# A second wait ahead of the indirect gathers in the hop loops of a graph kernel: Pool also waits for DVE's scores of the fifth group in front

## The reference, cut to what matters

```python
def agg(emb):
    a_input = jnp.concatenate([emb[head], emb[tail]], axis=-1)
    h = a_input @ fc_w.T + fc_b
    e = jnp.sum(h * rel_e, axis=-1)
    e = jnp.where(e > 0, e, LEAKY_SLOPE * e)
    m = jax.ops.segment_max(e, head, num_segments=N)
    ex = jnp.exp(e - m[head])
    denom = jax.ops.segment_sum(ex, head, num_segments=N)
    w = ex / denom[head]
    agg_emb = jax.ops.segment_sum(emb[tail] * w[:, None], head, num_segments=N)
    return agg_emb + emb
```

## Time and profile before

| What | Value |
|---|---|
| Runs shown | 9002.51 us median (8999.1 to 9027.76) |
| Time of the profiled execution | 8987.15 us |
| Its span, first to last instruction | 8985.1 us |
| Mean granted clock of PE | 0.782 of full speed |
| Busy share | PE 71%, DVE 54%, Pool 56%, ACT 25% |
| First and last gather of the hops (line 1305) | 2668.8 and 7368.5 us |
| Gathers of the hops | 2448 (3 x 408 x 2), 949 ns each |

### The profile page before, as it was taken

The page is one execution under the profiler, slowest core; times in us unless marked ns, Lnnn a source line. Parts: engine busy times, 40 slices in busy tenths (PEclk is TensorE's granted clock), DMA queues, the critical chain, the costliest instruction groups (busy, mean ns, idle before and its releaser), DMA issues. The chain is left out here.

```text
span 8985.1 us, 218235 instructions
## 1 busy us (share of the span) xinstructions
PE 6358.8 (71%) x51897; PEld 4355.0 (48%) x51899; DVE 4817.6 (54%) x20582; ACT 2235.8 (25%) x5532; POOL 5032.8 (56%) x4831
## 2 busy tenths in 40 slices
PE   2972888888208777788777588777787874666665
PEld 0110111111107666677666477666676763555554
DVE  7897555555315555555555555555555554333334
ACT  2000000000004444344444244434444431111111
POOL 2888777777764555455545355445455542555553
PEclk9985999999657888778888678788877775665655
DMA  3971666666223322223232233322222321222222
GB/s 124 310 233 41 195 186 191 186 186 192 44 49 82 83 82 82 80 83 83 82 80 80 63 81 83 82 80 81 81 84 81 83 61 38 48 47 48 47 47 40
DMA packets 573339, 882.86 MB, mean 98 GB/s; under 512 B 212594, under 2 KB 471113, under 8 KB 523997
## 3 DMA queue, kind: packets, MB, share of 16 engines
q10 hardware_dynamic: 76307, 411.51, 13.6%
q1 hardware_dynamic: 342522, 266.26, 11.2%
q0 software_dynamic: 154448, 204.37, 10.7%
HBM read 853.52 MB, written 20.36 MB: 97 GB/s over the span
## 5 line engine op out<-in xcount | busy, mean ns | idle before, releaser
L1305 POOL DMA_INDIRECT rows<-tab_d,stage_idx x2448 | 2322.7, 949 | 2378.7 <-PE ps_g L1369 1378.6
L232 POOL DMA_INDIRECT rec_d<-stage_rec,stage_row x1600 | 1967.5, 1230 | 648.8 <-issue 640.3
L440 PE MATMUL ps_gate<-ring,h_sb 128*1 128x512 f32 x3072 | 1530.8, 607 | 3.8 <-issue 3.6
L1332 PE MATMUL ps_t<-t_flat,hot_near 128*128 x9792 | 1247.3, 245 | 323.3 <-issue 313.5
L1369 PE MATMUL ps_g<-rows,rec_e 128*128 128x65 f32 x6528 | 1110.2, 325 | 505.1 <-ACT rec_e L1396 425.1
L1369 PEld LDWEIGHTS ps_g<-rows,rec_e 128*128 128x128 f32 x6528 | 1014.6, 237 | 584.3 <-issue 581.6
L1332 PEld LDWEIGHTS ps_t<-t_flat,hot_near 128*128 128x128 bf16 x9792 | 902.4, 111 | 633.3 <-issue 414.0
L1675 POOL DMA_INDIRECT t_flat<-y_d,stage_src x768 | 729.4, 950 | 814.6 <-issue 271.2
L1396 ACT ACTIVATE rec_e<-ps_p 128x512 f32<-128x512 f32 x816 | 485.8, 595 | 1965.2 <-remote 919.6
L672 DVE TENSOR_SCALAR lo_hot<-iota_b,lo_t 128x128 bf16<-128x128 bf16 x1568 | 445.3, 291 | 694.7 <-PE ps_deg L451 617.6
L1767 DVE TENSOR_SCALAR to_node<-wins_list,row_all 128x384 bf16<-128x384 bf16 x864 | 279.6, 336 | 921.8 <-remote 590.9
(11 more groups left out here) (341 smaller groups left out, 8076.3 us busy)
## 6 DMA issues: line engine op xcount, KB each, us to landing
rec_e<-lo_d SPq DMA_DIRECT2D x816, 256.0 KB
ring<-w_ih ACTq DMA_DIRECT2D x192, 1024.0 KB
ring<-w_hh ACTq DMA_DIRECT2D x192, 1024.0 KB
rows<-tab_d,stage_idx POOLq DMA_INDIRECT x2448
rec_e<-list_lo_d SPq DMA_DIRECT2D x216, 128.0 KB
rec_d<-stage_rec,stage_row POOLq DMA_INDIRECT x1600
t_flat<-y_d,stage_src POOLq DMA_INDIRECT x768
rec_d<-blank ACTq DMA_DIRECT2D x1, 3584.0 KB, 32.4
```

What stands on the lines that cost most here:

```text
L232: pool.indirect_dma_start(out=rec_d, out_offset=bass.IndirectOffsetOnAxis(ap=stage_row[:, h, j:j + 1], axis=0), in_=stage_rec[:, h, j, :], ...
L440: mm = pe.matmul(ps_gate[:, s, :], lhsT=h_sb[:, kc:kc + 1], rhs=ring[:, pc % RING, q, :], start=(kc == 0), stop=(kc == KC - 1))
L1305: pool.indirect_dma_start(out=rows[:, h * 4 + g, k, :], out_offset=None, in_=tab_d[hop], in_offset=bass.IndirectOffsetOnAxis(ap=stage_idx[ ...
L1332: mm = pe.matmul(ps_t[:, 0:TW], lhsT=hot_near[:, p, b, :], rhs=t_parts[:, ds(at + b, 1), j, :] .rearrange("p a c -> p (a c)"), start=False ...
```

## The change

Pool waits once more before the gathers of each group: group g's gathers also wait until DVE has written the scores of group g-5. The value is g-4, since `score_rdy` is 1 after group 0.

```diff
@@ -1296,10 +1296,12 @@
                         def half(it, h):
                             g0 = it * 8 + h * 4
                             wait_tick(pool, tick, summed, g0 - 7)
+                            wait_tick(pool, tick, score_rdy, g0 - 4)
                             wait_tick(pool, tick, staged[h], it * 16 + 16)
                             for g in range(4):
                                 if g:
                                     wait_tick(pool, tick, summed, g0 + g - 7)
+                                    wait_tick(pool, tick, score_rdy, g0 + g - 4)
                                 for k in range(1, KT):
                                     j = g * KT + k
                                     pool.indirect_dma_start(
```

## The result

The changed kernel takes 9144.6 us in the median of four runs (9135.64 to 9150.86), beside 9006.9 us for the kernel before on the same chip (four runs, 8999.1 to 9027.76). The ratio is 1.0148, with a 95% interval of 1.0129 to 1.0168: it is slower, by 138 us. The profiled execution took 9146.18 us (span 9144.1, granted clock 0.785 of full speed), 159 us more than that of before.

A forecast was written before the change was run, and what follows sets the result against it. It took a ring of Pool's gathers and PE's late signals, not PE's work, as the bound. +133 us in the hops and -8 at their starts gave +125 on 8987.15, 9112, plus 15 to the median: 9127 us; range 8980 to 9225.

The forecast's parts named there:

- The condition never binds: Pool's new score wait in the loop: met 3.2 us early in ordinary steps, 1.7 us early when gather groups run end to end.
- The ordinary step becomes 5.42 us: Pool's usual spacing of groups' first gathers: 5.27 us plus 0.15 us for the added computation and wait after `summed`.
- Pile-ups: Two groups' gathers end to end while PE's results reach others late: from one in 5.93 groups to 5.3, excess 1.88 us.
- +0.17 us for a group: Total slowdown taken per group in the two hops: 784 x 0.17 = +133 us, with ends +94 and +220.
- the upper end: Highest estimate of the hops' slowdown, from PE's mean need: 5.90 us per group, +0.28, or +220 us.
- PE's own need of 5.08 us: PE's time per group in the hops without its waits for ACT: (2230 - 215.0) / 397 = 5.08 us.
- the ring: Each hop step: three gathers 3.45 us, about 1.06 until PE's signals, about 0.75 until Pool's next gather, together 5.26 us.
- The hop's start, -4 us each: First groups of each hop: Pool pauses for scores, letting PE's results out; -8 us in all, ends 0 and -12.
- Rival (a): The wait separates gather groups that run end to end; every step 5.42 us, -157 us, about 8840 us; chance 0.16.
- Rival (b): The added wait and computation change nothing measurable in the hops; 9002 us; chance 0.15.
- Rival (c): Pool waits for a score of the same step; 6.9 us steps, up to 1000 us more, about 10000; chance 0.07.
- The rule of "SBUF — State Buffer": DVE's two-port operations block GpSimd's descriptor writes, so gathers moved behind scores would gain; at most 17 us.

The follow-up runs named there:

- seventh_in_front: The changed kernel with its second wait asking for the scores of group g-7 instead of g-5; 9139.06 us, ratio 1.0164 to the kernel before.
- score_wait_first: The changed kernel with its two waits swapped, the score wait ahead of `summed`; 8957.96 us, ratio 0.997 to the kernel before.
- two_gathers: Against the changed kernel: waits only for `x_rdy` of group g-4, and Pool's loop omits the fourth tile's gather (output wrong); 7702.78 us, ratio 0.8574 to before.
- x_rdy_then_score: The changed kernel with `x_rdy` of group g-4 replacing `summed` of g-8, score wait kept behind it; 8754.47 us, ratio 0.9743 to the kernel before.

## Why the prediction was right, step by step

I predicted 9127 us with a likeliest case of 9080 to 9225; the median is 9144.6. "Slower" was right, and so was the mechanism. Its steps:

- **The condition never binds.** Right for the loop. The shortest time from the end of a score to the first gather that it permits is 1.66 us in the changed trace, against the 1.7 expected, and `seventh_in_front` costs the same. At the starts of the hops it does bind, as said.
- **The ordinary step becomes 5.42 us.** Right: by position in the loop body the medians are 5.40 to 5.46 us, and 5.57 at the first, which now carries three waits. Before they were 5.24 to 5.30, and 5.42 and 5.34 at the halves' heads. `score_wait_first` shows that it is the pair's place that costs. That 0.16 and 0.07 us could be read from the two odd positions of the earlier trace rows was the useful part of the reading: the sequencer's own times are 0.157 and 0.096 us.
- **Pile-ups: one in 5.3 groups.** The right direction, too small. They are 83 and 86 in the 391 steps of each hop, one in 4.6 (before 67 and 71). The excess of a pile-up was right: 12.82 - 2 x 5.42 = 1.98 us at 3048.63 and 1.74 at 3239.11, against 1.88. With it, 5.42 + 1.88 / 4.6 = 5.83 us per group, as measured. So the term "+0.17 us for a group" was +0.20 (149 + 5 us over 784 groups), between the value taken and the upper end; the working itself gave 5.77 - 5.62 = 0.15, and the 0.02 on top were a leaning. The time between pile-ups was scaled from three steps of one of them, 0.75 us gained a step. That this was too coarse is my reading; no run tests it.
- **PE's own need of 5.08 us**, from which the upper end came, failed. I had subtracted only its waits for ACT from the pace; `two_gathers` runs at 4.04 us, which is under 4.9 us at the clock of before, by the estimate above. What gave way when the ring got shorter was mostly PE's busy time, as the granted clock rose. That the upper end (+0.28) still lay above the measured +0.20 was luck as far as it came from this figure.
- **The hop's start, -4 us each.** Mis-sized: group 16's first gather comes 2.9 and 2.5 us earlier, counted from group 0's. Groups 6 and 7 wait for scores as said, and group 8 starts 38.6 us after the first gather (2721.35) in place of 45.8. More than half of this lead of 7.2 us is lost again by group 16. `score_wait_first`, which pauses in the same way, keeps 3.7 and 7.1 us of it.
- **Rival (a)**, that the wait breaks the pile-ups, did not happen, since the condition is early. It priced the effect too low: with the permission taken from `x_rdy` there are hardly any, and the kernel is 3.4% faster, or 2.6% with the pair behind it (`x_rdy_then_score`, 233 us against the 157 said).
- **Rival (b)**, no difference, is what happens on a chip where PE's signals are not held back. I had not thought of the chip as a condition. That the result was measured on a chip of the kind that the rows come from was luck: on the other kind the forecast of +1.4% would have met +0.06%. On the chips of the first runs rival (b) is refuted by the ratio itself, and by `score_wait_first` (0.997) against `seventh_in_front` (1.0164) on one chip.
- **Rival (c)**, the scores in the ring: with the score one group nearer it comes, 5.4% slower. Its step was right (6.89 us), its price for the hops was not (6.27 us per group, not 6.9 throughout).
- **The rule of "SBUF — State Buffer"** in the Trainium skill gave nothing. The gathers' median is 944 ns and the longest 1074, a mean of 948 against 949, that is 2448 x 1 ns = 2 us at most.

## What to carry to other kernels

A wait that never binds is not free where the engine that waits is part of the ring that sets the pace: count what the issuing engine must do between the last signal that really arrives and the work it releases, and put every wait that is satisfied early, with its register arithmetic, ahead of the one that comes last. If an engine's early permission lets it issue two batches end to end and its neighbours stall, take the permission from a later signal; that was worth 3.4% on one of the slower chips, and nothing of it showed on the quick ones. And run a kernel on more than one chip before crediting a change, since what bounds it may not be there on the next.

## What the runs showed of the hardware

- On the chips where the kernel before takes 8980 to 9007 us, most of what PE has finished reaches DVE, ACT and Pool only after Pool's last back-to-back indirect gather. After three gathers the signals mostly come 0.9 to 1.3 us later (in hop 0 of the kernel before the median is 1.03 us for `summed` and 1.17 for `x_rdy`); after six end to end mostly 1.6 to 1.8, and the row shown starts 1.81 us after them (3242.55 to 3244.36), 5.8 us after PE's modelled end at 3238.54. Not every signal is held. Some still come out in the first microseconds of a run of gathers: `summed` comes 1.3 to 3.0 us after the first gather in 42 of the 59 runs of six in that hop, which is how a pile-up begins. On two others, where the kernel before takes 7112 to 7120 us, most signals come at once (0.04 us, 3001.16 to 3001.20). The Trainium skill says in "Perfetto Trace Analysis", under Tensor Engine Instruction, that the end of a TensorE row is an estimate and that the semaphore follows when PSUM has acknowledged the bytes. A delay of that kind fits the rows, which cannot show it directly.
- With the ring PE also gets less clock. In hop 0 the granted clock was 0.79 of full speed in the changed kernel (2720 to 4950 us), 0.99 for the same kernel on the quick chip (2720 to 4200 us), where PE pauses less, and 0.98 with two gathers a group (2720 to 4300 us). Over the whole run these are 0.785, 0.893 and 0.859.
- From one satisfied wait to the next Pool's sequencer takes 0.096 us, with a register computation between them 0.157 us; from the arrival of the signal to the start of an indirect gather it is 0.75 us, or 0.78 us from the end of DVE's row. "Advanced Engine Details and Errata" in the Trainium skill gives, under Network/Comms, 50 to 100 ns for reading a semaphore from a sequencer. The 96 ns, which take in the wait's own increment, lie within that.
